# Cross-attention and stream-mixing kernel: small work moved between units of the order, and one step from VectorE to GpSimd

## The chip, the cores and the metric

The kernel runs on one core of one Trainium2 chip. The metric is the device time of one execution in microseconds (us); lower is better. Each figure given for a kernel is the median of several executions.

## What is computed

Shapes: x and the context are 8 batches x 512 rows (D) x 2048 columns (S), all float32. The reference, cut to what matters:

```python
x = x + tanh(g_xattn) * xattn(layernorm(x), ctx, mask)
x = x + tanh(g_ffn) * ffn(layernorm(x))

def xattn(qk, v, masks):            # per window of 128 columns, 8 heads of 32
    q, k, val = Wq @ qk + bq, Wk @ qk + bk, Wv @ v + bv
    attn = softmax(where(mask, q.T @ k / sqrt(32), -1e9))
    return (Wo @ gelu(attn @ val) + bo) * masks

def ffn(x):                         # per row: 4 streams of 512 columns
    x_norm = x * rsqrt(mean(x * x) + eps)
    res, pre, post = x_norm @ W_res.T + .., x_norm @ W_pre.T + .., x_norm @ W_post.T + ..
    H = sinkhorn_log(res, 50 iterations, tau=0.1)      # 4 x 4 per row
    H_pre, H_post = softmax(pre), softmax(post)
    H = (1 - g) * I + g * H
    y = (sum_n x_n * H_pre_n) @ W_branch
    return H @ x_streams + y * H_post
```

## The kernel before, in words

**Units.** The program is one loop over a counter g, written out for every engine by itself; the engines meet only at semaphores. A unit g is one window of 128 columns with one group of four heads. Eight units are a chunk (512 columns), and r = g % 8 is the place in it; four chunks are a batch of 32 units. Attention takes the units 0 to 255; 16 units ahead of them prepare the first chunks, and some 60 behind them finish the last batches. In each unit TensorE makes transposed scores, one or more bank products, the scores of the next unit and the values of the one before; VectorE takes the maximum over the scores (L1035) and divides values by denominators (L1043); ScalarE exponentiates (L838), copies banks and forms the inverse denominators (L845, L847).

**Bank products.** `banked_at(g)` says which products fall on a unit: q and k projections of the next chunk (r = 0 to 3), values v (r = 6 and 7), output projection o of the chunk before (r = 4 and 5), transpositions and logits of the finished chunk, `pre` (transposition of xpre). They take turns in four PSUM banks, and a product waits until the bank's earlier content was read.

**High and low parts.** bfloat16 products carry a high and a low part. ScalarE makes the high part (`hi_ctx` L793, `hi_x` L806 behind `norm_x` L799, `hi_gelu` L863), and GpSimd subtracts it from the float32 value (`split_ctx` L476, `split_x` L471, `low_gelu` L482). The tables HI_X_AT, LOW_X_AT, HI_CTX_AT and LOW_CTX_AT hold the unit r for each of the four row tiles.

**Iterations.** The Sinkhorn iterations of a batch run in the background of the batch behind it, 26 units long (SINK), two iterations or four halves a unit. A half is: GpSimd scales the exponentials by the last factor (`scale`, L536, writes kp), VectorE sums (L1166, writes ssum) and takes the reciprocal (L1167, writes sa or sv). `scale_at(..., 0..3)` on GpSimd and `half_at(..., 0..3)` on VectorE stand between the other work of the unit, and both queues are in order. For the last batch VectorE scales too (L1156). When the iterations end, VectorE's `coefficients` makes the mixing matrix cmat and the constant ccon from kp (L1181 to L1191). A pause in the middle (RETURN) brings the factors back into the logarithms.

**Output tiles.** Each of the four row tiles of a batch is finished beside the next batch's attention: load of x1t, `first_products` (ScalarE), `make_xpre` (VectorE, L1201), transposition, two halves of the branch product, then ScalarE's `first_out` (L926), VectorE's `add_stream` (L1213) and `add_y` (L1229), and the stores. BESIDE and BEHIND hold each part's distance in units from TILE_AT; BEHIND serves the last two batches.

**Queues.** SP issues nearly all loads and stores in the order of its own loop, among them the load of xc for the chunk after next, which waits for the last `split_x` of the chunk in front of it. GpSimd's own queue carries `add_x`, which adds x to the attention result while it is moved.

## Time and profile before

| what | us |
|---|---|
| median of three runs (1875.27 to 1878.99) | 1876.54 |
| profiled execution, its own time | 1877.37 |
| its span | 1875.6 |
| TensorE busy in the span | 1407.9 |
| VectorE busy | 1410.1 |
| ScalarE busy | 1056.0 |
| GpSimd busy | 757.3 |

The profile is one execution of the program as the hardware profiler recorded it. Busy is the time in which at least one instruction of an engine ran; PE is TensorE's matmuls, PEld its weight loads, DVE is VectorE, ACT ScalarE, POOL GpSimd, SP the DMA queue of SyncE. Times in rows count from the start of the span. Idle time in brackets is that of the engine just before the instruction, with what ended it. The first maximum of unit 0 starts at 72.0 us and that of unit 255 at 1583.0 us, so 293 us lie behind the attention.

### The profile page before, as it was taken

What the parts mean: (1) busy time and instruction counts of PE and PEld (TensorE: products, weight loads), DVE (VectorE), ACT (ScalarE), POOL (GpSimd) and SP (SyncE); (2) the same over time, 40 slices, a digit from 0 to 9 for tenths busy, and PEclk for the clock granted to TensorE, in tenths of its full rate; (3) what the DMA queues carried; (4) which work ended last, traced back from release to release, by engine and by line L of the source; (5) the groups of instructions that cost most, each with busy time, mean ns of one, the idle gap of its engine ahead of it and who ended that gap; (6) DMA issues with size and microseconds to landing.
All of it is one profiled execution on the core that took longest, in us unless ns stands there. A gap on an engine that the chain in (4) does not pass through costs nothing.

```text
span 1875.6 us, 35269 instructions
## 1 busy us (share of the span) xinstructions
PE 1407.9 (75%) x12323; PEld 859.3 (46%) x12448; DVE 1410.1 (75%) x3678; ACT 1056.0 (56%) x2017; POOL 757.3 (40%) x1237
## 2 busy tenths in 40 slices
PE   2779999888988888888888788888888886521223
PEld 0546656555645454455555454445555553320111
DVE  3334555666788897888888888888778887779997
ACT  3557776666766666665666666655666664311111
POOL 3224334555454544455454535454454524320000
PEclk9889999999989998999999898989989997656656
DMA  8457765566656666666656566665665443411123
GB/s 258 137 153 193 218 179 161 160 182 186 179 155 184 188 177 187 188 189 182 185 157 181 164 185 174 176 188 164 170 174 168 120 125 90 124 66 69 56 84 118
DMA packets 173920, 299.85 MB, mean 160 GB/s; under 512 B 23568, under 2 KB 74640, under 8 KB 169648
## 3 DMA queue, kind: packets, MB, share of 16 engines
q1 hardware_dynamic: 156336, 264.03, 45.3%
q0 software_dynamic: 17408, 33.56, 10.2%
q8 instruction: 100, 1.64, 0.4%
q14 instruction: 76, 0.62, 0.1%
HBM read 179.81 MB, written 67.11 MB: 132 GB/s over the span
## 4 chain that ended last, share of the span: by engine, by line
PE 43%; DVE 24%; ACT 10%; POOL 9%; issue 9%; DMA 2%; SPq 2%; DVEq 0%; ACTq 0%; POOLq 0%
PE pr L611 10%; PE pr L625 7%; PE pr L638 6%; PE f L740 4%; DVE ssum L1166 4%; PE av_ps L725 4%; POOL kp L536 4%; DVE otile_odd L1213 3%; POOL ctx_hl L476 3%; DVE negm L1035 2%; PE av_ps L729 2%; DVE sa L1167 2%; PE s_ps L698 2%; DVE otile_even L1213 2%; SPq L404 2%
## 5 line engine op out<-in xcount | busy, mean ns | idle before, releaser
L1166 DVE TENSOR_REDUCE ssum<-kp 128x16 f32<-128x64 f32 x768 | 181.9, 237 | 183.2 <-POOL kp L536 178.1
L476 POOL TENSOR_TENSOR ctx_hl<-ctx_raw,ctx_hl 128x512 bf16<-128x512 f32 x128 | 149.6, 1174 | 219.8 <-ACT ctx_hl L793 219.8
L611 PE MATMUL pr<-x_hl,wq 128*128 128x512 bf16 x708 | 193.0, 425 | 43.9 <-POOL x_hl L471 36.0
L536 POOL TENSOR_TENSOR kp<-ke,sa 128x64 f32<-128x64 f32 x343 | 136.6, 398 | 220.0 <-DVE sa L1167 220.0
L1035 DVE TENSOR_REDUCE negm<-s_ps 128x4 bf16<-128x512 f32 x256 | 166.9, 652 | 73.6 <-PE s_ps L698 72.1
L536 POOL TENSOR_TENSOR kp<-ke,sv 128x64 f32<-128x64 f32 x329 | 145.3, 442 | 187.7 <-DVE sv L1167 187.0
L698 PE MATMUL s_ps<-k_st,q_st 97*128 97x128 bf16 x1024 | 104.3, 226 | 152.8 <-DVE negm L1035 138.6
L611 PE MATMUL pr<-x_hl,wk 128*128 128x512 bf16 x736 | 186.0, 406 | 13.1 <-DVE logit L1101 8.0
L638 PE MATMUL pr<-o_sb,wo 128*128 128x512 bf16 x735 | 185.6, 389 | 11.5 <-POOL o_sb L482 6.9
L838 ACT ACTIVATE probs<-st_ps,key_bias 128x512 f32<-128x512 f32 x256 | 173.5, 678 | 30.5 <-PE st_ps L712 30.2
L471 POOL TENSOR_TENSOR x_hl<-xc,x_hl 128x512 bf16<-128x512 f32 x128 | 148.6, 1161 | 92.3 <-ACT x_hl L806 92.3
L625 PE MATMUL pr<-wv,ctx_hl 128*128 128x256 bf16 x1536 | 181.4, 276 | 3.2 <-DVE wv L1250 3.2
L845 ACT ACTIVATE lnden<-av_ps 128x128 f32<-128x128 f32 x256 | 71.1, 278 | 197.0 <-PE av_ps L729 191.9
L698 PEld LDWEIGHTS s_ps<-k_st,q_st 97*128 97x128 bf16 x1024 | 71.7, 100 | 223.1 <-DVE negm L1035 153.5
L625 PEld LDWEIGHTS pr<-wv,ctx_hl 128*128 128x128 bf16 x1536 | 148.0, 99 | 27.6 <-issue 10.0
L710 PE MATMUL st_ps<-q_st,k_st 96*128 96x128 bf16 x1024 | 148.3, 222 | 5.2 <-ACT probs L838 5.0
L685 PE MATMUL pr<-id_sb,xpre 128*128 128x128 f32 x128 | 24.5, 325 | 169.6 <-DVE xpre L1201 169.6
L1213 DVE SCALAR_TENSOR_TENSOR otile_even<-x1t_even,cmat,otile_even 128x512 f32<-128x512 f32 x192 | 147.7, 780 | 1.6 <-ACT otile_even L926 1.2
L1213 DVE SCALAR_TENSOR_TENSOR otile_odd<-x1t_odd,cmat,otile_odd 128x512 f32<-128x512 f32 x192 | 148.2, 794 | 0.7
L712 PE MATMUL st_ps<-id_bf,negm 128*128 128x128 bf16 x1024 | 147.4, 221 | 0.0
L725 PE MATMUL av_ps<-probs,v_t 128*32 128x128 f32 x2048 | 117.6, 303 | 36.2 <-DVE o_sb L1043 35.2
L611 PEld LDWEIGHTS pr<-x_hl,wq 128*128 128x128 bf16 x768 | 78.8, 108 | 141.7 <-issue 46.7
(142 smaller groups left out, 3047.1 us busy)
## 6 DMA issues: line engine op xcount, KB each, us to landing
xs<-in_dram SPq DMA_DIRECT2D x128, 256.0 KB, 4.6
xc<-in_dram SPq DMA_DIRECT2D x32, 1024.0 KB, 10.6
ctx_raw<-in_dram SPq DMA_DIRECT2D x32, 1024.0 KB, 6.8
x1c<-in_dram POOLq DMA_DIRECT2D x64, 512.0 KB, 9.3
x_dram<-x1c SPq DMA_DIRECT2D x32, 1024.0 KB, 4.9
q_st<-q_hl SPq DMA_DIRECT2D x384, 64.0 KB
k_st<-k_hl SPq DMA_DIRECT2D x384, 64.0 KB
x1t_even<-x_dram SPq DMA_DIRECT2D x16, 1024.0 KB, 5.8
```

What stands on the lines that cost most here:

```text
L471: nc.gpsimd.tensor_tensor(x_hl[:, G % 2, 1, t, :], xc[:, t, :], x_hl[:, G % 2, 0, t, :], ALU.subtract).then_inc(x_split, 1)
L476: ins = nc.gpsimd.tensor_tensor(ctx_hl[:, 1, t, :], ctx_raw[:, t, :], ctx_hl[:, 0, t, :], ALU.subtract)
L536: nc.gpsimd.tensor_tensor(kp[:], ke[:], v, ALU.mult).then_inc(kp_made, 1)
L611: ins = nc.tensor.matmul(bank(what)[:], w[:, a, t, i * P:(i + 1) * P], x_hl[:, G % 2, m, t, :], start=(t == 0 and a + m == 0), stop=(t == ...
L625: ins = nc.tensor.matmul(bank(what)[:, j * E:(j + 1) * E], ctx_hl[:, a, t, win], wv[:, m, t, :], start=(t == 0 and a + m == 0), stop=(t == ...
L638: ins = nc.tensor.matmul(bank(what)[:], wo[:, a, et, t * P:(t + 1) * P], o_part(G, et, m), start=(et == 0 and a + m == 0), stop=(et == ET ...
L698: ins = nc.tensor.matmul(s_ps[:, h * W:(h + 1) * W], q_st[0:ROWS + 1, G % 2, et, h, win], k_st[0:ROWS + 1, G % 2, et, h, win], start=True, ...
L725: nc.tensor.matmul(av_ps[rows, 0:W], v_t[:, G % 2, w, et * P + h * DH:et * P + (h + 1) * DH], probs[:, k % 2, h * W:(h + 1) * W], start=Tr ...
L838: nc.scalar.activation(probs[:, k % 2, :], st_ps[:], ACT.Exp, bias=key_bias[:, b, w:w + 1], scale=SCALE).then_inc(exp_done, 1)
L1035: nc.vector.tensor_reduce(negm[:, k % 2, :], s_ps[:].rearrange("p (h j) -> p h j", h=HPT), AX.X, ALU.max, negate=True).then_inc(max_done, 1)
L1166: cf.link(nc.vector.tensor_reduce(s_t, k, AX.X, ALU.add))
L1213: ins = nc.vector.scalar_tensor_tensor(out=otile[n % 2][:, i, :], in0=x1t[n % 2][:, j * C:(j + 1) * C], scalar=cmat[:, f % 2, t, i, j:j + ...
```

## The change

- ScalarE: high parts of ctx and x, `first_products` and `first_out` move from behind the unit's bank copies to a place ahead of them.
- GpSimd: low context parts come at r = 1, 2, 2, 3 instead of 0, 1, 1, 4, the first low part of x at r = 3 instead of 2, both low gelu parts at r = 4 instead of 3. Inside a unit the context split and the split of x change places, so that the split of x stands behind the third kp. The adds `add_x` move from r = 6 and 7 to r = 7 and the r = 0 that follows.
- `coefficients` runs on GpSimd in unit COEF_AT, the one behind the last iteration, with the row sum as two additions of halves and without the first scaling, which kp holds already. The semaphore for `pre` is now its own, and VectorE's next softmax, which reuses kp, waits for the coefficients.
- Bank products: v at r = 4 and 7, o at r = 5 and 6, logits at r = 5, `pre` two units behind xpre instead of one. Statistics at r = 2 and 5, the selection, the iterations and the output tiles one unit later, the pieces of the statistics of x at other units.

```diff
@@ -53,11 +53,11 @@
-HI_X_AT, LOW_X_AT = [1, 4, 5, 6], [2, 5, 6, 7]
-HI_CTX_AT, LOW_CTX_AT = [0, 0, 1, 1], [0, 1, 1, 4]
-
-T_AT, LOGITS_AT, SELECT_AT = [3, 3, 4, 4], 7, 8
-STAT_B_AT = [1, 3]
+HI_X_AT, LOW_X_AT = [1, 4, 5, 6], [3, 5, 6, 7]
+HI_CTX_AT, LOW_CTX_AT = [0, 0, 1, 1], [1, 2, 2, 3]
+
+T_AT, LOGITS_AT, SELECT_AT = [3, 3, 4, 4], 5, 9
+STAT_B_AT = [2, 5]
...
+COEF_AT = SINK_AT + len(SINK)
...
-BESIDE = dict(load=-8, first=-6, xpre=-5, pre=-4, branch_0=0, branch_1=1, out_0=-1, out_1=0,
+BESIDE = dict(load=-8, first=-6, xpre=-5, pre=-3, branch_0=0, branch_1=1, out_0=-1, out_1=0,
...
-TILE_AT = {(f, t): UNITS * (f + 1) + 53 + UPC * t for f in range(LAST_BESIDE + 1) for t in range(DT)}
+TILE_AT = {(f, t): UNITS * (f + 1) + 54 + UPC * t for f in range(LAST_BESIDE + 1) for t in range(DT)}
...
-    return [UNITS * (b - 1) + UPC * (p // 4 - 2) + 2 * (p % 4) for p in range(XS)]
+    return [UNITS * (b - 1) + UPC * (p // 4 - 2) + (1, 3, 4, 5)[p % 4] for p in range(XS)]
...
-                 6: [("v", G + 1, 0)], 7: [("v", G + 1, 1)]}.get(r, [])
-    if 0 <= G - 1 < NG and r in (4, 5):
-        made += [("o", G - 1, 2 * (r - 4)), ("o", G - 1, 2 * (r - 4) + 1)]
+                 4: [("v", G + 1, 0)], 7: [("v", G + 1, 1)]}.get(r, [])
+    if 0 <= G - 1 < NG and r in (5, 6):
+        made += [("o", G - 1, 2 * (r - 5)), ("o", G - 1, 2 * (r - 5) + 1)]
...
-                if r == 1 and 0 <= G - 2 < NG:
+                if r == 2 and 0 <= G - 2 < NG:
...
+            def coefficients(f):
+                pool.wait_ge(scale_made, HALVES * (f + 1))
+                flat = kp[:].rearrange("p t i j -> p t (i j)")
+                cp.link(nc.gpsimd.tensor_tensor(kp[:], kp[:], bcast(sv[:], 2, N), ALU.mult))
+                cp.link(nc.gpsimd.tensor_scalar(flat, flat, gt[:, 2:3], None, ALU.mult))
+                cp.link(nc.gpsimd.tensor_tensor(flat, flat, bcast(eye_g[:], 1, DT), ALU.add))
+                cp.link(nc.gpsimd.tensor_scalar(flat, flat, gt[:, 1:2], None, ALU.mult))
+                cp.link(nc.gpsimd.tensor_tensor(rows2[:], kp[:, :, :, 0:2], kp[:, :, :, 2:4], ALU.add))
+                cp.link(nc.gpsimd.tensor_tensor(rows1[:], rows2[:, :, :, 0], rows2[:, :, :, 1], ALU.add))
+                cp.link(nc.gpsimd.tensor_tensor(flat, flat, bcast(rb[:, f % 3, 3, :], 2, N * N), ALU.mult))
+                nc.gpsimd.tensor_tensor(ccon[:, f % 2], rows1[:], bcast(rb[:, f % 3, 6, :], 2, N), ALU.mult
+                                        ).then_inc(coef_ready, 1)
+                nc.gpsimd.tensor_tensor(cmat[:, f % 2].rearrange("p t i j -> p t (i j)"), flat,
+                                        bcast(eye_sb[:], 1, DT), ALU.add).then_inc(coef_ready, 1)
...
+                for ready in ffn_at(g, COEF_AT):
+                    coefficients(ready)
...
+                for H, t in at_step(g, -1, LOW_CTX_AT):
+                    split_ctx(H, t)
+                if 0 <= G - 1 < NG and r == 4:
+                    low_gelu(G - 1, 0)
+                scale_at(f, its, 2)
+                if 0 <= G - 1 < NG and r == 4:
+                    low_gelu(G - 1, 1)
                 for H, t in at_step(g, -2, LOW_X_AT):
                     split_x(H, t)
-                if 0 <= G - 1 < NG and r == 3:
-                    low_gelu(G - 1, 0)
-                scale_at(f, its, 2)
-                if 0 <= G - 1 < NG and r == 3:
-                    low_gelu(G - 1, 1)
-                for H, t in at_step(g, -1, LOW_CTX_AT):
-                    split_ctx(H, t)
                 scale_at(f, its, 3)
-                if 0 <= G - 1 < NG and r in (6, 7):
-                    add_x(G - 1, r - 6)
+                if 0 <= G - 1 < NG and r == 7:
+                    add_x(G - 1, 0)
+                if 0 <= G - 2 < NG and r == 0:
+                    add_x(G - 2, 1)
...
-                    act.wait_ge(coef_ready, 2 * f + 1)
+                    act.wait_ge(pre_ready, f + 1)
...
+                for H, t in at_step(g, -1, HI_CTX_AT):
+                    hi_ctx(H, t)
+                for H, t in at_step(g, -2, HI_X_AT):
+                    norm_x(H, t)
+                    hi_x(H, t)
+                for done, t in tiles_at(g, "first"):
+                    first_products(done, t)
+                for pair in range(2):
+                    for done, t in tiles_at(g, f"out_{pair}"):
+                        first_out(done, t, pair)
...
-                for H, t in at_step(g, -1, HI_CTX_AT):
-                    hi_ctx(H, t)
-                for H, t in at_step(g, -2, HI_X_AT):
-                    norm_x(H, t)
-                    hi_x(H, t)
...
-                for done, t in tiles_at(g, "first"):
-                    first_products(done, t)
-                for pair in range(2):
-                    for done, t in tiles_at(g, f"out_{pair}"):
-                        first_out(done, t, pair)
...
+                if f:
+                    dve.wait_ge(coef_ready, 2 * f)
...
-                if half and it == ITERS - 1:
-                    dve.wait_ge(scale_made, HALVES * (f + 1))
-                    coefficients(f)
```

ScalarE in unit 153 (r = 1 of a chunk with iterations). Before:

```order
L838 ACTIVATE probs<-st_ps,key_bias 128x512
L917 ACTIVATE xpt<-pr 128x512
L845 ACTIVATE lnden<-av_ps 128x128
L847 ACTIVATE rden<-lnden 128x128
L820 ACTIVATE q_hl<-pr,bq_sb 128x512
L793 ACTIVATE ctx_hl<-ctx_raw 128x512 x2
L799 ACTIVATE xc<-xc,ra 128x512
L806 ACTIVATE x_hl<-xc 128x512
```

With the change:

```order
L862 ACTIVATE probs<-st_ps,key_bias 128x512
L817 ACTIVATE ctx_hl<-ctx_raw 128x512 x2
L823 ACTIVATE xc<-xc,ra 128x512
L830 ACTIVATE x_hl<-xc 128x512
L844 ACTIVATE q_hl<-pr,bq_sb 128x512
L869 ACTIVATE lnden<-av_ps 128x128
L871 ACTIVATE rden<-lnden 128x128
```

The two high context parts (ctx_hl) and the normalization of x (xc, x_hl) stood behind the copy of the q bank and now stand ahead of it; xpt, the copy of `pre`, has left this unit.

GpSimd where two low context parts meet, units r = 1 and 2 before:

```order
L536 TENSOR_TENSOR kp<-ke,sv 128x64
L536 TENSOR_TENSOR kp<-ke,sa 128x64
L536 TENSOR_TENSOR kp<-ke,sv 128x64
L476 TENSOR_TENSOR ctx_hl<-ctx_raw,ctx_hl 128x512 x2
L536 TENSOR_TENSOR kp<-ke,sa 128x64
L536 TENSOR_TENSOR kp<-ke,sv 128x64
L536 TENSOR_TENSOR kp<-ke,sa 128x64
L471 TENSOR_TENSOR x_hl<-xc,x_hl 128x512
L536 TENSOR_TENSOR kp<-ke,sv 128x64
```

With the change (they are now in r = 2):

```order
L540 TENSOR_TENSOR kp<-ke,sa 128x64
L540 TENSOR_TENSOR kp<-ke,sv 128x64
L540 TENSOR_TENSOR kp<-ke,sa 128x64
L480 TENSOR_TENSOR ctx_hl<-ctx_raw,ctx_hl 128x512 x2
L540 TENSOR_TENSOR kp<-ke,sv 128x64
L540 TENSOR_TENSOR kp<-ke,sa 128x64
```

The pair ctx_hl stood between the third and the fourth kp of its unit and now stands between the second and the third.

GpSimd at the end of the last batch's work, with the change:

```order
L552 TENSOR_TENSOR kp<-kp,sv 128x64
L553 TENSOR_SCALAR kp<-kp,gt 128x64
L554 TENSOR_TENSOR kp<-kp,eye_g 128x64
L555 TENSOR_SCALAR kp<-kp,gt 128x64
L556 TENSOR_TENSOR rows<-kp 128x32
L557 TENSOR_TENSOR rows<-rows 128x16
L558 TENSOR_TENSOR kp<-kp,rb 128x64
L559 TENSOR_TENSOR ccon<-rows,rb 128x16
L561 TENSOR_TENSOR cmat<-kp,eye_sb 128x64
```

These nine (the coefficients) were VectorE's.

## Rows read from the trace of the kernel before

**Rows 1.** page, busy time of each engine (us, share of the span, count)
```profile
PE 1407.9 (75%) x12323; PEld 859.3 (46%) x12448; DVE 1410.1 (75%) x3678; ACT 1056.0 (56%) x2017; POOL 757.3 (40%) x1237
```

**Rows 2.** busy us of each engine by batch of 32 units; then granted clock, DMA share, GB/s
```profile
382.00:568.00 186.00, 160.28 (x1523) 99.94 (x1539) 136.53 (x399) 122.69 (x240) 94.11 (x167) 0.95 0.63 176
568.00:772.00 204.00, 171.71 (x1538) 105.05 (x1553) 172.77 (x447) 131.30 (x252) 100.11 (x167) 0.93 0.64 181
772.00:980.00 208.00, 175.17 (x1537) 105.96 (x1552) 172.61 (x447) 131.21 (x252) 100.31 (x167) 0.92 0.63 179
...
1391.00:1583.00 192.00, 156.93 (x1410) 96.35 (x1425) 154.15 (x408) 113.12 (x219) 81.74 (x142) 0.90 0.49 136
1583.00:1876.00 293.00, 91.37 (x287) 47.19 (x288) 248.17 (x689) 58.97 (x101) 36.03 (x82) 0.63 0.27 86
```

**Rows 3.** the same for the four chunks of the batch at 772 to 980 us
```profile
772.00:822.00 50.00, 42.65 (x378) 25.21 (x381) 42.47 (x108) 32.90 (x64) 24.22 (x38) 0.93 0.67 191
822.00:880.00 58.00, 46.48 (x391) 28.05 (x393) 47.30 (x136) 33.83 (x66) 31.45 (x64) 0.88 0.65 186
880.00:927.00 47.00, 41.81 (x391) 26.34 (x393) 39.59 (x89) 31.74 (x63) 17.10 (x22) 0.96 0.60 169
927.00:980.00 53.00, 44.23 (x385) 26.36 (x388) 43.26 (x117) 32.74 (x60) 27.54 (x45) 0.90 0.58 168
```

**Rows 4.** waits over the whole span: who for whom, us, times, longest
```profile
POOL ctx_hl L476 <- ACT ctx_hl L793: 219.8, 61, 19.2
...
DVE ssum L1166 <- POOL kp L536: 178.1, 304, 4.4
```

**Rows 5.** timeline, unit r = 1 of the chunk at 927 us
```profile
936.83 4.70 PE L611 MATMUL pr<-x_hl,wq 128*128 128x512 bf16 x11 [0.33 <-issue]
...
942.85 1.17 POOL L476 TENSOR_TENSOR ctx_hl<-ctx_raw,ctx_hl 128x512 bf16<-128x512 f32 x1 [4.62 <-ACT ctx_hl L793]
...
943.97 0.30 POOL L536 TENSOR_TENSOR kp<-ke,sa 128x64 f32<-128x64 f32 x1
...
944.30 0.27 DVE L1166 TENSOR_REDUCE ssum<-kp 128x16 f32<-128x64 f32 x1 [4.33 <-POOL kp L536]
...
945.45 0.40 PE L698 MATMUL s_ps<-k_st,q_st 97*128 97x128 bf16 x4 [0.87 <-DVE negm L1035]
```

**Rows 6.** timeline, VectorE in unit r = 3 of that chunk
```profile
954.40 0.22 DVE L1166 TENSOR_REDUCE ssum<-kp 128x16 f32<-128x64 f32 x1 [1.30 <-POOL kp L536]
```

**Rows 7.** timeline, collisions of GpSimd and VectorE in unit r = 4
```profile
959.94 0.66 DVE L1213 SCALAR_TENSOR_TENSOR otile_even<-x1t_even,cmat,otile_even 128x512 f32<-128x512 f32 x1
...
960.10 0.65 POOL L536 TENSOR_TENSOR kp<-ke,sv 128x64 f32<-128x64 f32 x1 [0.96 <-DVE sv L1167]
...
960.72 1.15 POOL L476 TENSOR_TENSOR ctx_hl<-ctx_raw,ctx_hl 128x512 bf16<-128x512 f32 x1
...
961.21 1.21 DVE L1213 SCALAR_TENSOR_TENSOR otile_even<-x1t_even,cmat,otile_even 128x512 f32<-128x512 f32 x1
```

**Rows 8.** timeline, end of the last batch's iterations
```profile
1810.38 0.23 DVE L1181 TENSOR_TENSOR kp<-ke,sa 128x64 f32<-128x64 f32 x1
...
1812.46 0.22 DVE L1191 TENSOR_TENSOR cmat<-kp,eye_sb 128x64 f32<-128x64 f32 x1
```

**Rows 9.** timeline, VectorE behind unit 256, two reciprocals 15 units apart
```profile
1584.19 0.25 DVE L1167 RECIPROCAL sa<-ssum 128x16 f32<-128x16 f32 x1
...
1667.25 0.25 DVE L1167 RECIPROCAL sa<-ssum 128x16 f32<-128x16 f32 x1
```

**Rows 10.** page, DMA issues: operation, count, KB each, us to landing
```profile
xc<-in_dram SPq DMA_DIRECT2D x32, 1024.0 KB, 10.6
```

**Rows 11.** timeline, load of xc, two context parts, first activation of the next unit r = 1
```profile
769.42 0.38 SPq L366 DMA_DIRECT2D xc<-in_dram  x1
...
776.00 1.13 ACT L793 ACTIVATE ctx_hl<-ctx_raw 128x512 bf16<-128x512 f32 x2
...
777.04 0.67 ACT L838 ACTIVATE probs<-st_ps,key_bias 128x512 f32<-128x512 f32 x1
```

More of the change, by code:

```diff
@@ L220, in program @@
         ones = sb("ones", [P, P])
[L221 removed]
+        spare = sb("spare", [P, 3])
         csum = sb("csum", [P, NL])
@@ L245, in program @@
         ccon = sb("ccon", [P, 2, DT, N])
+        rows2 = sb("rows2", [P, DT, N, 2])
+        rows1 = sb("rows1", [P, DT, N])
         pre = sb("pre", [P, 3, DT, N])
@@ L332, in program @@
         y_read = sem("y_read")
+        pre_ready = sem("pre_ready")
         coef_ready = sem("coef_ready")
```

22 lines of the change are left out of this document (4 added, 18 removed).

## The prediction, on record before the changed kernel ran

> **What bounds the kernel now.** I read the engine totals first, then the same totals batch by batch and chunk by chunk, then the waits, and last the timeline inside single units. The totals show two engines level: TensorE and VectorE are each busy for 75% of the span, ScalarE for 56%, GpSimd for 40% [rows 1]. By batch it is the same picture, sharper: in the batch at 772 to 980 us TensorE is busy for 175.2 and VectorE for 172.6 of 208 us [rows 2]. Neither is full, so some 33 us of this batch are lost in handshakes between them. The four chunks of that batch take 50, 58, 47 and 53 us for nearly equal TensorE work (42 to 46 us) [rows 3]; the loss sits in some units of a chunk and not in others.
>
> The list of waits names it. GpSimd waits 219.8 us for ScalarE's high part of the context, and VectorE waits 178.1 us for the scaled matrix kp that GpSimd makes [rows 4]. These are one chain, as unit r = 1 shows: TensorE's q projection starts at 936.83 and takes 4.70 us, ScalarE copies that bank at its end, and only behind this copy come the free activations that make the high context parts; GpSimd had waited 4.62 us for one of those, and since its queue is in order the kp behind the split starts at 943.97. VectorE stood still for 4.33 us, the maximum of the next unit was late, and TensorE idled another 0.87 us before its scores [rows 5]. So TensorE's own result, which nobody in the chain needed, holds TensorE. Unit r = 3 has a smaller copy of it (1.30 us) behind the low part of the gelu [rows 6]. In front of r = 1 TensorE works at the lower level: 11 matmuls took 4.70 us [rows 5], and the granted clock of the batch is 0.92 of the 2.4 GHz level [rows 2].
>
> **The change, part by part.**
> (1) ScalarE's free work ahead of bank copies, and low context parts a unit later (units 1, 2, 2, 3 instead of 0, 1, 1, 4), low gelu in unit 4. GpSimd then finds its operand ready each time. In the chunk at 927 to 980 us this removes 4.33 [rows 5] and 1.30 us [rows 6], and about 0.7 us of the same in r = 0, whose split moves away too (estimate: a sixth of the 4.33): 6.3 us. What is late next is kp itself. In r = 2 two splits of 1.17 us [rows 5] now stand between two kp; VectorE has a reduction (0.27) and one add (0.66) to cover them: 2 x 1.17 - 0.93 = 1.4 us of wait. Bounds: 0 if a bank read covers it, 2.3 if nothing does.
> (2) The splits of x move behind the third kp of their unit. What that costs is shown in r = 4: an add of VectorE with two SBUF inputs takes 0.66 us by itself and 1.21 us when it starts inside GpSimd's 1.15 us split; in the other direction kp takes 0.65 us beside the add and 0.30 us without it [rows 5, 7]. Before the change the split of x ran beside bank reads in units 5 to 7; now VectorE's add follows. Three units x 0.55 us = 1.7 us per chunk given back (bounds 0 and 7 x 0.55 = 3.9). The Trainium skill (SBUF — State Buffer, on the shared port pair) says that a VectorE instruction with two SBUF inputs and a GpSimd instruction that reads SBUF lock each other out until the first has ended. The trace agrees: the add ends 0.55 us behind the split's end. The rule speaks against this change, because GpSimd is freed to run just where VectorE runs.
> Net of (1) and (2) for this chunk: -6.3 + 1.4 + 1.7 = -3.2 us.
> (3) Coefficients on GpSimd. VectorE loses a chain of nine instructions, 1810.38 to 1812.68, 2.3 us [rows 8], seven times beside the last batch's. The same unit also held four adds of y and TensorE's two selections; the second selection and the statistics move on by one unit, which I put at 1.2 us (estimate, about half of the 2.3). So the chunk at 822 to 880 us wins 3.2 + 2.3 + 1.2 = 6.7 us. On GpSimd the nine take 0.30 us each [rows 5] and a handshake of about 0.1: some 3.6 us, in unit 17, where no kp is asked for: hidden. If GpSimd were late there, the softmax of unit 18 would wait, since it now asks for the coefficients.
> (4) Values at 4 and 7, output projection at 5 and 6, logits at 5, the transposition of xpre two units behind it instead of one: TensorE's heavy units are spread, and no wait for xpre is left at r = 0. TensorE's sum is unchanged. I count nothing beyond (1), as VectorE sets the pace then.
> The chunk at 772 to 822 us has a pause in its iterations, so I count -4.4 + 3.1 = -1.3 us; the chunk at 880 to 927 us has hardly any, and a third of its idle 47 - 39.6 us [rows 3] gives -2.5. The batch: -3.2 - 6.7 - 1.3 - 2.5 = -13.7 us. I take four fifths, -11 us, since new small waits appear when four engines move closer.
> Other batches, scaled by their load [rows 2]: the one at 568 us, whose row stands for the two behind 980 us as well, -10 each; 382 to 568 us, with few output tiles, -7; 218 to 382 us -2; the first 0; the last at 1391 us, -9. Sum: -11 - 30 - 7 - 2 - 9 = -59 us.
> (5) Behind unit 256, 293 us with VectorE busy for 248 [rows 2]. Iterations, tiles and statistics all start a unit later, so one iteration unit moves behind unit 256. Fifteen such units took 1667.25 - 1584.19 = 83.1 us, 5.5 us each [rows 9]. The coefficients of the batch before the last leave VectorE there (-2.3 us), and those of the last one, which ScalarE's first output waits for, take 3.6 us on GpSimd instead of 2.3 [rows 5, 8], +1.3. Sum +4.5 us.
> Total: -59 + 4.5 = -54.5 us against the profiled execution's 1877.4, so 1822.9; the median of the three runs lies 0.8 us lower: **1822 us**. The Trainium skill (GPSIMD Engine Reference, Engine selection) says to keep elementwise work on VectorE, as GpSimd is about twice as slow with two inputs. By it the last coefficients would cost 4.6 us instead of 3.6, 1 us more in the sum; for the small kp the row shows 0.30 us against VectorE's 0.23, so the trace does not agree at this size.
>
> **The rivals.**
> A, the forecast: the chain is broken, collisions and r = 2 give half of it back. For it: in units 5 to 7 of today's chunks, where no split waits for ScalarE, TensorE hardly idles. 1822 us.
> B, it all comes: no collision, no wait in r = 2. Then the chunk gains 6.3 instead of 3.2; with 3.1 us more in three chunks of four, over some five batches' worth, that is 37 us more at four fifths: 1785 us. Against it: the collisions in rows 7.
> C, the collisions cost their upper bound: 2.2 us more per chunk of this kind, and the wait in r = 2 grows to 2.3: 3.1 us more, so that a chunk hardly gains: 1822 + 37 = 1859 us. By the skill's lock (same page as above) this is the case that follows if every split meets an add; the sentences above say what rows show of it.
> D, slower: ScalarE now reaches the normalization of xc before its bank copies. Today it gets there late, because the copy of q waits for TensorE. The load of xc is issued at 769.42 and takes 10.6 us (median) to land, 780.0; the exponential of r = 1 starts at 777.04, and two context parts (1.13 us) now follow its 0.67 us: ScalarE is there at 778.8 [rows 10, 11]. The load is released by the last split of x, which now stands one kp later (about 1.5 us): 781.5, a wait of 2.7 us with the bank copy and the inverse denominators behind it, and VectorE's division and TensorE's values behind those. Over 27 chunks 73 us, if nothing covers it: 1895 us. It decides from 54.5 / 27 = 2.0 us exposed per chunk. Against it: GpSimd is no longer late, so the split comes earlier in time, and the division has most of a unit of slack.
> E, the pace is set by a loop that the chain only hides, and the time stays: 1877 us.
>
> **How the numbers follow.** A 0.60, own range 1803 to 1845; B 0.12; C 0.15; D 0.09; E 0.04. The range takes in A, C but for its worst part, and the near half of B: 1788 to 1860 us. A difference under about 0.2% (3.7 us) can't be told from none. Faster by more than that: A, B, C, 0.87; within it: E, 0.04; slower: D, 0.09.
>
> **What the changed profile would show.** (1) right: GpSimd's wait for ScalarE's ctx_hl near 0 in the main part and VectorE's wait of 4.3 us in r = 1 gone; wrong if it has moved to another split. (2) right: adds of about 1.2 us in units 5 to 7, and one wait of 1 to 2 us for kp in r = 2. (3) right: the unit with the coefficients no longer than its neighbours, nine small GpSimd instructions in unit 17 that nobody waits for. (5) right: the part behind unit 256 4 to 6 us longer. D would show as waits of ScalarE's xc for the DMA, with TensorE's values late behind them. The prediction is wrong if VectorE's busy time, not its idle time, takes what the waits gave back, beyond the 3.9 us per chunk of the bound.

## Result and profile after

| kernel | median, us | range | executions |
|---|---|---|---|
| before | 1876.24 | 1874.94 to 1878.99 | 6 |
| changed | 1868.22 | 1865.97 to 1870.83 | 6 |

The ratio is 0.9956, 95% interval 0.9943 to 0.9969: the change makes the kernel 8 us faster, where 54 were forecast. The sign was right, and 1868 lies outside the range of 1788 to 1860. The profiled execution's span is 1866.9 us.

Engine totals of the page, then the busy time by stretch (columns as in [rows 2]): first the same two stretches of time as there, then the four chunks of the batch that answers to [rows 3]. In the changed kernel the maximum of unit 255 starts at 1568.4 us and the span ends at 1866.9, so the stretch from 1583 us holds less of its work than it did before.

```profile
PE 1410.8 (76%) x12448; PEld 864.1 (46%) x12448; DVE 1410.7 (76%) x3606; ACT 1055.8 (57%) x2017; POOL 807.8 (43%) x1309
```

```profile
772.00:980.00 208.00, 177.01 (x1591) 108.18 (x1590) 176.49 (x447) 134.25 (x258) 109.05 (x179) 0.93 0.64 183
1583.00:1876.00 293.00, 88.13 (x224) 42.06 (x224) 236.54 (x649) 54.18 (x91) 38.34 (x91) 0.61 0.24 83
...
771.20:822.00 50.80, 42.27 (x382) 25.47 (x380) 42.59 (x108) 32.64 (x63) 25.69 (x38) 0.93 0.63 182
822.00:874.90 52.90, 42.87 (x383) 25.62 (x382) 45.76 (x126) 34.27 (x68) 30.64 (x56) 0.94 0.61 175
874.90:924.80 49.90, 43.84 (x398) 28.29 (x397) 40.78 (x92) 31.26 (x63) 23.53 (x40) 0.90 0.64 183
924.80:975.80 51.00, 44.64 (x396) 26.79 (x396) 44.43 (x116) 33.02 (x62) 28.42 (x45) 0.93 0.64 183
```

VectorE's total is that of [rows 1], and it holds 72 instructions less. The chunk with the coefficients went from 58 to 53 us and the one at 927 us from 53 to 51, but the light chunk, which had the least idle time [rows 3], went from 47 to 50. This batch takes 204.6 us where it took 208; three waits of the whole span show that the chain of [rows 4] was broken all the same:

```profile
PE s_ps L722 <- DVE negm L1060: 155.8, 74, 4.9
...
DVE ssum L1193 <- POOL kp L540: 123.8, 301, 2.5
...
POOL ctx_hl L480 <- ACT ctx_hl L817: 54.6, 14, 13.7
```

GpSimd's wait for the context parts fell from 219.8 to 54.6 us, VectorE's for kp from 178.1 to 123.8; TensorE's wait for the maxima rose from 138.6 (the line below, of the kernel before) to 155.8.

```profile
PE s_ps L698 <- DVE negm L1035: 138.6, 90, 4.0
```

The timeline of the units r = 1 to 3 of the same chunk (answers to [rows 5]):

```profile
936.58 0.63 DVE L1060 TENSOR_REDUCE negm<-s_ps 128x4 bf16<-128x512 f32 x1
...
937.95 2.72 POOL L480 TENSOR_TENSOR ctx_hl<-ctx_raw,ctx_hl 128x512 bf16<-128x512 f32 x2
...
938.96 0.60 PE L682 MATMUL pr<-id_sb,x1c 128*128 128x128 f32 x4
...
940.96 0.22 DVE L1193 TENSOR_REDUCE ssum<-kp 128x16 f32<-128x64 f32 x1 [1.30 <-POOL kp L540]
...
944.29 0.61 PE L722 MATMUL s_ps<-k_st,q_st 97*128 97x128 bf16 x4 [4.73 <-DVE negm L1060]
...
945.95 1.11 PE L682 MATMUL pr<-id_sb,x1c 128*128 128x128 f32 x4
```

In r = 1 VectorE no longer stands still before its maximum; the wait of 4.33 us is gone. In r = 2 the pair of context splits makes it wait 1.30 us, where 1.4 was forecast. TensorE then has too little of its own to do and idles 4.73 us, and its next four transpositions take 1.11 us instead of 0.60: the granted clock is 0.50 there, the lower of its two levels (1.2 GHz), and 1.00 at the earlier four.

For the comparisons below I measure a unit from one maximum of VectorE to the next, as the mean over the batches 3 to 6 (counted from 0) of the profiled execution, and sum eight units to a chunk:

| us per chunk, units | before | f1 | g2 | g3 | g4 | changed | e3 |
|---|---|---|---|---|---|---|---|
| 0 to 7 | 49.8 | 47.0 | 45.5 | 46.8 | 48.0 | 50.7 | 49.8 |
| 8 to 15 | 56.6 | 53.3 | 50.5 | 51.0 | 51.8 | 52.9 | 51.7 |
| 16 to 23 | 46.9 | 43.4 | 46.0 | 47.3 | 52.4 | 49.9 | 48.7 |
| 24 to 31 | 52.3 | 47.9 | 47.9 | 48.7 | 48.5 | 50.7 | 51.0 |
| batch | 205.6 | 191.5 | 190.0 | 193.8 | 200.8 | 204.2 | 201.1 |

### The profile page after: what moved, and what is told of

The parts are those of the page before. It is cut to its first block, busy times and chain, and to the rows that moved or that the text cites. A ratio compares the mean times of both kernels' runs of the same rounds, so it can differ in the third digit from the quotient of the medians.

```text
span 1866.9 us, 35401 instructions
## 1 busy us (share of the span) xinstructions
PE 1410.8 (76%) x12448; PEld 864.1 (46%) x12448; DVE 1410.7 (76%) x3606; ACT 1055.8 (57%) x2017; POOL 807.8 (43%) x1309
## 4 chain that ended last, share of the span: by engine, by line
DVE 34%; PE 26%; POOL 16%; issue 11%; ACT 5%; DMA 4%; SPq 3%; POOLq 0%; DVEq 0%; ACTq 0%
POOL kp L540 8%; PE pr L635 7%; DVE ssum L1193 6%; PE pr L649 4%; DVE sa L1194 3%; DVE negm L1060 3%; DMA xc<-in_dram 3%; DVE bn_b L1095 3%; DVE xpre L1210 3%; PE pr L682 3%; DVE otile_odd L1222 3%; POOL ctx_hl L480 3%; PE pr L662 2%; DVE otile_even L1222 2%; PE av_ps L749 2%
## 5 line engine op out<-in xcount | busy, mean ns | idle before, releaser
L1193 DVE TENSOR_REDUCE ssum<-kp 128x16 f32<-128x64 f32 x768 | 181.5, 236 | 128.9 <-POOL kp L540 123.8
L540 POOL TENSOR_TENSOR kp<-ke,sa 128x64 f32<-128x64 f32 x343 | 151.1, 441 | 273.3 <-DVE sa L1194 273.3
L540 POOL TENSOR_TENSOR kp<-ke,sv 128x64 f32<-128x64 f32 x329 | 151.2, 460 | 265.6 <-DVE sv L1194 258.7
L722 PE MATMUL s_ps<-k_st,q_st 97*128 97x128 bf16 x1024 | 106.6, 230 | 171.7 <-DVE negm L1060 155.8
L635 PE MATMUL pr<-x_hl,wk 128*128 128x512 bf16 x768 | 198.0, 413 | 0.0
L480 POOL TENSOR_TENSOR ctx_hl<-ctx_raw,ctx_hl 128x512 bf16<-128x512 f32 x128 | 153.5, 1223 | 54.6 <-ACT ctx_hl L817 54.6
L1222 DVE SCALAR_TENSOR_TENSOR otile_odd<-x1t_odd,cmat,otile_odd 128x512 f32<-128x512 f32 x192 | 163.9, 876 | 0.6
L1222 DVE SCALAR_TENSOR_TENSOR otile_even<-x1t_even,cmat,otile_even 128x512 f32<-128x512 f32 x192 | 158.2, 834 | 4.6 <-ACT otile_even L950 4.3
L709 PE MATMUL pr<-id_sb,xpre 128*128 128x128 f32 x128 | 34.0, 421 | 154.1 <-DVE xpre L1210 154.1
L764 PE MATMUL f<-wb,xpt 128*128 128x512 f32 x256 | 143.3, 696 | 5.5 <-ACT xpt L941 5.5
```

The costliest lines, as they stand in the source:

```text
L480: ins = nc.gpsimd.tensor_tensor(ctx_hl[:, 1, t, :], ctx_raw[:, t, :], ctx_hl[:, 0, t, :], ALU.subtract)
L540: nc.gpsimd.tensor_tensor(kp[:], ke[:], v, ALU.mult).then_inc(kp_made, 1)
L635: ins = nc.tensor.matmul(bank(what)[:], w[:, a, t, i * P:(i + 1) * P], x_hl[:, G % 2, m, t, :], start=(t == 0 and a + m == 0), stop=(t == ...
L722: ins = nc.tensor.matmul(s_ps[:, h * W:(h + 1) * W], q_st[0:ROWS + 1, G % 2, et, h, win], k_st[0:ROWS + 1, G % 2, et, h, win], start=True, ...
L1193: cf.link(nc.vector.tensor_reduce(s_t, k, AX.X, ALU.add))
L1222: ins = nc.vector.scalar_tensor_tensor(out=otile[n % 2][:, i, :], in0=x1t[n % 2][:, j * C:(j + 1) * C], scalar=cmat[:, f % 2, t, i, j:j + ...
```

## Experiments

Eighteen kernels. Those of one group (e, f, g, k1 to k4, k5 and k6) share a chip and its runs of the kernel before; differences in us between groups are of the medians, and the ratios with their 95% intervals say how far they hold. Many expectations missed; where a time lies outside what was expected, the text says so. Two theories stood at the start: the forecast gain never came, because the chain of waits was worth less than it looked; or it came, and other parts of the change took it back.

**e1 to e4: the changed kernel with one part altered.**

e1, low context parts one unit earlier:

```diff
-HI_CTX_AT, LOW_CTX_AT = [0, 0, 1, 1], [1, 2, 2, 3]
+HI_CTX_AT, LOW_CTX_AT = [0, 0, 1, 1], [1, 1, 2, 3]
```

> The changed kernel with the second low context part in unit r = 1 instead of r = 2 (LOW_CTX_AT 1, 1, 2, 3). Theory S (the split pair of r = 2 is what stands in the way: VectorE waits 1.3 us for kp there, TensorE has run ahead and starves 4.7 us before the scores of r = 3, its clock falls to 1.2 GHz): the wait of r = 2 goes, since r = 1 has 1.45 us of xpre work between the second and the third half, 1.0 us per chunk or more, over 28 chunks 25 to 50 us: 1820 to 1845 us. Theory P (TensorE's own load in r = 3 sets the time of r = 3 and 4): 1860 to 1870 us, the wait only moves.

Measured: 1867.11 us, ratio 0.9938 (0.9916 to 0.9960): no different from the changed kernel, inside the 1860 to 1870 of theory P. Unit 2 of a batch shrinks from 7.0 to 5.9 us and unit 1 grows from 6.0 to 7.0: the wait only moves. The pair in r = 2 is not the loss.

e2, `pre` moved from r = 3 to r = 4 (transposition three units behind xpre):

```diff
-BESIDE = dict(load=-8, first=-6, xpre=-5, pre=-3, ...
+BESIDE = dict(load=-8, first=-6, xpre=-5, pre=-2, ...
```

> The changed kernel with the transposition of xpre in unit r = 4 instead of r = 3 (pre=-2 in BESIDE), so that r = 3 holds two transpositions and k, and r = 4 two transpositions, pre and v. Theory P: the copy of the k bank comes 1.1 us earlier in r = 3, VectorE's wait of 1.65 us for it in r = 4 shrinks to under 0.6 us: 1.1 us in some 24 chunks, 1842 to 1850 us. Theory S: TensorE only starves a little longer before r = 4, 1863 to 1870 us.

Measured: 1861.73 us, 0.9912 (0.9891 to 0.9933). Some 6 us, the intervals of the ratios overlap, and the time lies between the two expectations; the place of `pre` is a small part at most.

e3, second half of the statistics at r = 4:

```diff
-STAT_B_AT = [2, 5]
+STAT_B_AT = [2, 4]
```

> The changed kernel with the second half of the statistics in r = 4 instead of r = 5 (STAT_B_AT 2, 4), so that GpSimd's last chain of small statistics work falls on unit 15 and no longer on unit 16, where the chain for the statistics of x stands too. Theory G (two chains of small GpSimd instructions between two kp cost 2.47 us once per batch): the wait in unit 16 halves, 1.2 us in 7 batches, 1858 to 1862 us. Theory that these chains are covered by TensorE's selections there: 1866 to 1870 us.

Measured: 1852.46 us, 0.9860 (0.9836 to 0.9885), 16 us less than the changed kernel and below both expectations. One small piece in the wrong unit costs twice what the whole change gained: unit 5 of a batch is 7.9 us long in the changed kernel and 5.5 here, while unit 4 grows from 6.3 to 7.7. STAT_AT follows this table, and so does where GpSimd computes the inverse roots. In the changed kernel those of x (ra) and of the streams (rb) both fall on unit 16:

```profile
875.37 0.63 POOL L500 TENSOR_TENSOR ra<-ra 128x4 f32<-128x4 f32 x1
...
878.52 0.20 POOL L534 TENSOR_TENSOR rb<-rb 128x4 f32<-128x4 f32 x1
878.67 0.30 POOL L540 TENSOR_TENSOR kp<-ke,sa 128x64 f32<-128x64 f32 x1
...
879.00 0.26 DVE L1193 TENSOR_REDUCE ssum<-kp 128x16 f32<-128x64 f32 x1 [2.47 <-POOL kp L540]
```

Eleven tiny instructions, 3.4 us in a row in front of a kp, and VectorE waits 2.47 us. In e3 unit 16 is 6.8 us long instead of 8.0, the 1.2 us that was expected. The batch as a whole shrinks by 3.1 us, so most of the gain lies in other units.

e4, coefficients on VectorE again, all else as changed:

```diff
-                for ready in ffn_at(g, COEF_AT):
-                    coefficients(ready)
...
+                if half and it == ITERS - 1:
+                    dve.wait_ge(scale_made, HALVES * (f + 1))
+                    coefficients(f)
```

> The changed kernel with the coefficients made by VectorE again, behind the last iteration of unit 16. By the term of the prediction (2.3 us seven times, on VectorE's path) it is 16 us slower, less 1.3 us that it gains at the very end: 1883 us. If the coefficients on GpSimd were nearly worthless (TensorE's selections set units 15 to 18): 1866 to 1870 us.

Measured: 1898.65 us, 1.0107 (1.0084 to 1.0129), slower than the kernel before and 15 us above the 1883 expected. Thirty us for a chain of nine instructions, seven times, is more than the chain lasts (2.3 us each). Unit 16 of a batch is 16.0 us long here and 8.0 in the changed kernel, while unit 18 falls from 10.7 to 8.2. The timeline of GpSimd and VectorE at the end of unit 16:

```profile
891.59 1.24 POOL L494 DMA_DIRECT2D x1c<-in_dram  x1 [0.19 <-issue]
892.43 4.90 POOL L480 TENSOR_TENSOR ctx_hl<-ctx_raw,ctx_hl 128x512 bf16<-128x512 f32 x4
...
896.88 1.56 POOL L475 TENSOR_TENSOR x_hl<-xc,x_hl 128x512 bf16<-128x512 f32 x1
```

```profile
892.88 5.65 DVE L1189 TENSOR_TENSOR kp<-ke,sa 128x64 f32<-128x64 f32 x1
898.57 0.23 DVE L1190 TENSOR_TENSOR kp<-kp,sv 128x64 f32<-128x64 f32 x1
```

The first product of the coefficients takes 5.65 us where it took 0.23 [rows 8]. It begins while GpSimd works through five splits in a row and ends with them. So about 5.4 us of the unit's 8 are this hold-up and 2.3 the chain itself. In front of the row stands the issue of `add_x` (x1c), 0.84 us ahead of the first split.

**f1 to f4: single parts on the kernel before, and one taken out of the changed kernel.**

f1, only ScalarE's order (`hi_ctx`, `norm_x`, `hi_x`, `first_products`, `first_out` ahead of the bank copies):

> The kernel before with ScalarE's part of the change alone: high parts of ctx and x, first_products and first_out ahead of the bank copies. The chain of the prediction (TensorE's q projection, bank copy, context part, split, kp) is cut by this alone: by its price (4.3 us in r = 1, 1.3 in r = 3 not, 28 chunks) 1876 - 3.5 x 28 x 0.8 = about 1800 us. Theory T (cutting the chain mostly moves the waiting: TensorE starves elsewhere, and an unblocked GpSimd holds VectorE up at the shared port): 1860 to 1880 us.

Measured: 1802.03 us, 0.9588 (0.9569 to 0.9607).

f2, only the low parts later:

```diff
-HI_X_AT, LOW_X_AT = [1, 4, 5, 6], [2, 5, 6, 7]
-HI_CTX_AT, LOW_CTX_AT = [0, 0, 1, 1], [0, 1, 1, 4]
+HI_X_AT, LOW_X_AT = [1, 4, 5, 6], [3, 5, 6, 7]
+HI_CTX_AT, LOW_CTX_AT = [0, 0, 1, 1], [1, 2, 2, 3]
```

> The kernel before with the low context parts at r = 1, 2, 2, 3 and the first low part of x at r = 3 alone. GpSimd then finds its operands ready without ScalarE's new order: the wait of 4.3 us in r = 1 goes too, about the same time as with ScalarE's part alone by both theories: near 1800 us by the price of the chain, 1860 to 1880 us by theory T.

Measured: 1813.64 us, 0.9661 (0.9638 to 0.9684): 63 us less than before, nearer to the price of the chain than to theory T.

f3, only `coefficients` on GpSimd, with the semaphores it needs:

> The kernel before with the coefficients on GpSimd alone, in the unit behind the last iteration. By the term of the prediction -2.3 x 7 + 1.3: 1861 us. By the run with the coefficients back on VectorE (30 us slower than the changed kernel, one of VectorE's nine instructions held for 5.65 us behind GpSimd's run of context splits) the move is worth much only where GpSimd's splits run free beside it; in the kernel before they wait for ScalarE there, so again about 1861 us, not 1846.

Measured: 1870.66 us, 0.9963 (0.9947 to 0.9978): 6 us less than before, where 15 were expected.

f4, the changed kernel with GpSimd's old order inside a unit:

```diff
                 scale_at(f, its, 1)
+                for H, t in at_step(g, -2, LOW_X_AT):
+                    split_x(H, t)
-                for H, t in at_step(g, -1, LOW_CTX_AT):
-                    split_ctx(H, t)
...
-                for H, t in at_step(g, -2, LOW_X_AT):
-                    split_x(H, t)
+                for H, t in at_step(g, -1, LOW_CTX_AT):
+                    split_ctx(H, t)
```

> The changed kernel with the old order inside a unit on GpSimd: the split of x behind the second kp, the context split behind the third. The collisions of the split of x with VectorE's adds (0.55 us in r = 3, 5, 6, 7) go, the pair of context splits in r = 2 stands behind an add and the statistics and costs less. If collisions and the pair are what the gain was given back to: -2.5 us per chunk, 1868 - 50 = 1815 us. If TensorE's pace is what is left: 1860 to 1868 us.

Measured: 1837.75 us, 0.9774 (0.9751 to 0.9798), 30 us less than the changed kernel and between the two expectations.

The first theory falls with f1: ScalarE's order alone brings 74 us, more than the whole forecast. Its four chunks, to be read beside [rows 3]:

```profile
755.70:802.00 46.30, 41.05 (x382) 24.90 (x380) 42.77 (x107) 32.42 (x63) 25.41 (x38) 0.96 0.74 205
802.00:855.60 53.60, 45.17 (x388) 27.21 (x386) 47.37 (x135) 33.02 (x65) 32.17 (x63) 0.90 0.69 197
855.60:899.40 43.80, 40.08 (x390) 25.10 (x390) 39.60 (x92) 32.23 (x64) 18.90 (x24) 1.00 0.63 181
899.40:947.40 48.00, 44.00 (x400) 26.89 (x399) 43.51 (x117) 32.64 (x61) 28.44 (x45) 0.93 0.67 192
```

VectorE's busy times are those of before, TensorE's are 0.2 to 1.7 us shorter at a higher granted clock; each chunk lost 3 to 5 us, the light one included. It is the chain: of the 14.1 us that a batch gains, 12.8 lie in the four units r = 1, where GpSimd had waited for the context parts (9.6, 9.6, 10.5 and 10.2 us before, 6.5, 6.5, 7.6 and 6.5 in f1). f1 moves four kinds of work at once, which were not tried apart, but f2 touches only the splits, brings 63 us and adds only 7 to g1: f1 and f2 break the same chain, each at one end.

**g1 to g4: the change put together step by step**, all four on one chip. g1 is f1 with the coefficients of f3; g2 adds the tables of f2; g3 adds GpSimd's new order (f4's edit the other way round); g4 adds values at 4 and 7, output projection at 5 and 6, logits at 5, the low gelu in unit 4, and the store and adds that go with them. What then still lacks is the shift by a unit of statistics, selection, iterations and tiles, with `pre` and the pieces of the statistics of x.

> ScalarE's new order (1802 us alone) and the coefficients on GpSimd, nothing else of the change; first of four kernels that build the change up step by step. Coefficients alone gave 6 us: 1796 us. If an unblocked GpSimd makes the coefficients' move worth more (VectorE held at the shared port), below 1790; if GpSimd's chain of nine stands in front of kp-free splits that TensorE waits for, 1802 to 1806.

> The same with the low context parts at r = 1, 2, 2, 3 and the first low part of x at r = 3. Both cures of the one chain together: if there was only one wait to remove, no further gain, within 5 us of the step before; if waits for ScalarE were still left in r = 0 and r = 1, 10 to 15 us less.

> The same with GpSimd's new order inside a unit (context split behind the second kp, split of x behind the third). By the run with the old order in the changed kernel (30 us faster) this step costs 25 to 35 us. If that order only hurts together with the new bank places, under 10 us.

> The same with v at r = 4 and 7, o at r = 5 and 6, logits at r = 5, low gelu at r = 4 and the adds of x at r = 7 and 0. What is left to the changed kernel behind this one is the shift of selection, statistics, iterations and tiles by a unit. The steps from 1802 to 1868 us must add up to 66: if TensorE's crowding in r = 3 and 4 is the cost, it comes with the shift (pre into r = 3) and not here, and this step is within 5 us; if the bank places themselves cost, 10 to 20 us here.

| step | us | ratio, interval | step's own |
|---|---|---|---|
| f1: ScalarE's order | 1802.0 | 0.9588 (0.9569 to 0.9607) | -74 |
| g1: + coefficients | 1804.5 | 0.9605 (0.9582 to 0.9629) | +2 |
| g2: + low parts later | 1797.1 | 0.9555 (0.9532 to 0.9578) | -7 |
| g3: + GpSimd's order | 1818.1 | 0.9675 (0.9652 to 0.9699) | +21 |
| g4: + banks, low gelu | 1847.7 | 0.9836 (0.9813 to 0.9859) | +30 |
| changed: + shift | 1868.2 | 0.9956 (0.9943 to 0.9969) | +21 |

The second theory stands: the gain came in the first three steps, and the last three give nearly all of it back. g2 beats both kernels. The first and the last row are from other chips than g1 to g4; by the ratios the steps are -77, +3, -9, +23, +30 and +22 us. g1 lies where the chain of nine on GpSimd was expected to stand in the way (1802 to 1806), g2's step of -7 lies between its two expectations, g3's is a little under the 25 to 35 expected, and g4's is above both of its expectations.

In g4 the loss sits in few units. Against g3, unit 17 grows from 11.4 to 14.4 us, unit 22 from 7.3 to 9.4, unit 4 from 7.0 to 8.2, and the last unit of each chunk (7, 15, 23, 31) from 5.4 or 5.6 to 6.3. GpSimd and VectorE in unit 17 of g4:

```profile
873.13 1.24 POOL L493 DMA_DIRECT2D x1c<-in_dram  x1 [0.25 <-issue]
873.97 4.92 POOL L479 TENSOR_TENSOR ctx_hl<-ctx_raw,ctx_hl 128x512 bf16<-128x512 f32 x4
878.44 1.56 POOL L474 TENSOR_TENSOR x_hl<-xc,x_hl 128x512 bf16<-128x512 f32 x1
```

```profile
873.32 0.75 DVE L1043 SCALAR_TENSOR_TENSOR q_hl<-pr,bq_sb,q_hl 128x512 bf16<-128x512 f32 x1 [1.99 <-ACT q_hl L843]
873.99 7.23 DVE L1219 SCALAR_TENSOR_TENSOR otile_odd<-x1t_odd,cmat,otile_odd 128x512 f32<-128x512 f32 x2
881.14 1.27 DVE L1093 BATCH_NORM_STATS2 bn_b<-x1c 128x6 f32<-128x512 f32 x2
```

It is e4's picture with another victim: two adds of 0.66 us take 7.23, and again `add_x` is issued 0.84 us ahead of the row. In unit 22 ScalarE is late: the copy of the values' bank and that of the logits now stand in front of the exponentials of the iterations:

```profile
906.21 0.57 ACT L900 ACTIVATE lgs<-pr 128x512 f32<-128x512 f32 x1
...
907.20 0.24 ACT L916 ACTIVATE ke<-zl 128x64 f32<-128x64 f32 x1
```

```profile
907.47 0.22 DVE L1191 TENSOR_REDUCE ssum<-ke 128x16 f32<-128x64 f32 x1 [2.83 <-ACT ke L916]
```

g3 waits 0.76 us at this place. In the changed kernel the picture differs, since its softmax and coefficients stand a unit later: no add of a batch 3 to 6 lasts over 1.72 us there. Its long units are 16 (8.0 us, 3.4 in g4) and 18 (10.7, 4.5 in g4), while 17 has 4.1 us and 22 has 4.8.

**k1 to k6: why the bank step costs 30 us.**

k1, g2 with g4's bank step and GpSimd's old order:

> ScalarE's order, coefficients on GpSimd, low parts later, and the moved banks and logits, but GpSimd's old order inside a unit (g2 plus the step of g4). In g4 unit 17 takes 14.4 us: VectorE's two adds last 7.23 us behind five GpSimd splits in a row. Pile-up theory (the bank step costs only because GpSimd's splits then run in a row beside VectorE's adds, which the new order in a unit brings): at most 10 us over g2, 1797 to 1807, and no add over 2.5 us. Bank theory (the places of values, output projection and logits cost by themselves, through TensorE's clock and waits): about 30 us over g2, 1822 to 1830.

Measured: 1841.16 us, 0.9786 (0.9772 to 0.9799), 44 us over g2. The bank step costs by itself, more than either theory gave it, so the pile-up theory falls as I had put it. Its second half, no add over 2.5 us, was wrong too: the two adds of unit 17 take 7.88 us here. The hold-up comes with the bank step, not with GpSimd's order. And from here to g4 that order costs only 7 us, where it cost 21 behind g2.

k2, g4 with values at 6 and 7 and output projection at 4 and 5, and with the store and the adds of x that go with them:

```diff
-                 4: [("v", G + 1, 0)], 7: [("v", G + 1, 1)]}.get(r, [])
-    if 0 <= G - 1 < NG and r in (5, 6):
-        made += [("o", G - 1, 2 * (r - 5)), ("o", G - 1, 2 * (r - 5) + 1)]
+                 6: [("v", G + 1, 0)], 7: [("v", G + 1, 1)]}.get(r, [])
+    if 0 <= G - 1 < NG and r in (4, 5):
+        made += [("o", G - 1, 2 * (r - 4)), ("o", G - 1, 2 * (r - 4) + 1)]
```

> g4 with the values at units 6, 7 and the output projection at 4, 5 again (with the store and the adds of x that go with them); logits at 5 and the low gelu in unit 4 stay. If the moved values and output projection carry the 30 us: about 1820. If the logits or the gelu do: about 1845.

Measured: 1831.13 us, 0.9727 (0.9709 to 0.9745). 17 us less than g4, between the two expectations. Unit 17 is 11.8 us and its adds 2.3 us for two: without the move no add is held up that long. But the move that k2 takes back includes that of `add_x` from r = 0 to r = 6, so k2 does not tell the banks' places from the place of this issue.

k3, g4 with `LOGITS_AT` 7:

> g4 with the logits at unit 7 again. The logits' bank lies in unit 21 of a batch, where g4's units 20 to 22 are 4 us longer than g3's (units 22: 9.4 against 7.3). If the logits' place does that: 15 to 20 us less than g4's 1848, some 1830. If not: 1845 to 1850.

Measured: 1847.01 us, 0.9814 (0.9794 to 0.9833). The logits cost nothing; unit 22 stays at 9.1, so its length is not theirs. In k2 it is 7.8, so it comes with values and output projection, which were not moved apart.

k5, g4 with both low parts of the gelu at r = 3:

> g4 with the low gelu in unit 3 of GpSimd again. Of g4's 30 us over g3 the places of values and output projection carry 16.5 (k2) and the logits none (k3). Unit 4 of a chunk is 8.2 us long in k2, k3 and g4 alike, against 7.0 in g3. If the gelu does that: about 12 us less than g4, some 1836. If the parts only cost together: 1845 or more.

Measured: 1857.02 us, 0.9893 (0.9871 to 0.9914): 9 us more than g4, not the 12 less that the gelu alone would give. The gelu's place depends on the banks': beside the moved banks unit 4 is the better, while beside the old ones gelu and logits together cost 13 us (k2 against g3; 10 by the ratios). So the parts cannot be priced one by one.

k6, g4 with a wait more, so that the splits of unit 17 start behind the adds:

```diff
+                if g >= 0 and u == 17 and b >= 3:
+                    pool.wait_ge(out_ready, 8 * (b - 3) + 7)
                 for H, t in at_step(g, -1, LOW_CTX_AT):
                     split_ctx(H, t)
```

> g4, and in unit 17 of the last five batches GpSimd waits for VectorE's first pair of output adds before it begins its splits. In g4 two adds take 7.23 us there beside five splits in a row, 1.3 to 1.5 us by themselves. Starvation theory (back-to-back GpSimd instructions keep the add from starting): an added wait makes the kernel faster, the adds at 0.7 us each, unit 17 some 4 to 5 us shorter, five times: 1822 to 1832 against g4's 1848. Rival (the unit waits for TensorE's q bank or for something else anyway, the long adds only fill the wait): 1845 or more.

Measured: 1840.90 us, 0.9807 (0.9788 to 0.9825). GpSimd and VectorE in unit 17:

```profile
878.77 4.49 POOL L479 TENSOR_TENSOR ctx_hl<-ctx_raw,ctx_hl 128x512 bf16<-128x512 f32 x4 [2.05 <-DVE otile_odd L1221]
```

```profile
877.27 1.41 DVE L1221 SCALAR_TENSOR_TENSOR otile_odd<-x1t_odd,cmat,otile_odd 128x512 f32<-128x512 f32 x2
...
879.79 0.71 DVE L1126 SCALAR_TENSOR_TENSOR logit<-csum,rb,pr 128x32 f32<-128x32 f32 x4
880.53 3.89 DVE L1136 SCALAR_TENSOR_TENSOR logit<-logit,rb,base_sb 128x32 f32<-128x32 f32 x4
```

The adds now run ahead of GpSimd's row and take 1.41 us for two again, so beside the row they lost the time. The wait also parts the row from the issue of `add_x`, which now lies 3.3 us ahead of it (875.48 us). But the row now meets the logits, which took 0.74 us and take 3.89. Unit 17 falls from 14.4 to 12.2 us, and the time lies between the two expectations. Its interval overlaps g4's, so that the wait makes the kernel faster is shown by the unit, not by the time.

k4, f1 with f2's tables, coefficients on VectorE:

> The kernel before with ScalarE's order and the later low parts only; coefficients stay on VectorE. Coefficients cost 2.5 us on top of ScalarE's order and 5.6 less than before alone, so their own effect here should be within 5 us of g2's 1797: 1792 to 1800. If GpSimd's pile-up of splits met the coefficient chain on VectorE as in the changed kernel (30 us), it would be 1810 or more.

Measured: 1806.95 us (1798.57 to 1812.33), 0.9611 (0.9593 to 0.9630), outside the 1792 to 1800 expected; g2 stays the best. By the medians the coefficients on GpSimd are thus worth 6 us on the kernel before, nothing on f1, some 10 on top of k4 (k4 to g2) and 30 in the changed kernel. The profiled executions of k4 and g2 differ by 1.5 us only, and show why the move brings so little: VectorE reaches unit 17 of this batch 3.6 us earlier in g2 (854.20 us) than in k4 (857.80), but TensorE, behind its selections, starts the q projection at 855.10 against 854.75. VectorE waits for its bank:

```profile
859.33 0.75 DVE L1041 SCALAR_TENSOR_TENSOR q_hl<-pr,bq_sb,q_hl 128x512 bf16<-128x512 f32 x1 [3.15 <-ACT q_hl L841]
```

Units 15 to 17 together take 20.1 us in k4 and 20.2 in g2.

## Why the prediction was wrong

**Term 1, the chain: right, and larger than forecast.** Taking the collisions out of the forecast (1.7 of the 3.1 us that made 37 in rival B, so 20 us), and the later statistics (1.2 us a batch, some 5 us in all), terms 1 and 3 say 59 + 20 - 5 = 74 us; g2, which has both, gained 79 against the 1876 of before. That this fits so well is partly luck. Without the coefficients (2.3 us a batch, some 13 in all) the chain was put at about 61 us, and k4, which has the chain without the coefficients, gained 69 (73 by its ratio) and f1 alone 74. The coefficients cost 2 us on top of f1 and brought 10 on top of k4, of which the two traces show 1.5. In single places the working holds: the wait in r = 2 is 1.30 us, 1.4 forecast, and the chunk with the pause, put at 4.4 without a working, gave 4.3 in g2. But the light chunk gave 3.5 us in f1 where I had put 2.5.

**Term 2, the collisions: the size right on g2, the mechanism in part.** 20 us forecast, 21 measured (g2 to g3). But the same edit costs 7 us behind k1 and 30 in the changed kernel (f4), so the match is of one neighbourhood. Adds of 1.21 us stand in units 5 and 6 as foreseen, none in unit 7, and those of unit 1 got shorter: all stretched adds of a batch together make 1.4 us of the 3.8 that g3's batch is longer. What the rest is was not tried.

**Term 3, the coefficients: wrong.** It was priced at 2.3 us each time, 16 in all; the runs gave 6, -2, 10 and 30. VectorE is free 2.4 us earlier in unit 15 (7.8 us in f1, 5.4 in g1), but unit 17 grows from 7.6 to 11.5, where TensorE, not VectorE, comes last. In the changed kernel most of the gain is that of avoiding the hold-up beside GpSimd's row (e4). Only the chain's own length came out: on GpSimd the last coefficients take 3.3 us, 3.6 forecast:

```profile
1800.36 0.30 POOL L552 TENSOR_TENSOR kp<-kp,sv 128x64 f32<-128x64 f32 x1 [135.97 <-DVE sv L1194]
...
1803.37 0.32 POOL L561 TENSOR_TENSOR cmat<-kp,eye_sb 128x64 f32<-128x64 f32 x1
```

**Term 4 is the step that failed: "I count nothing beyond (1), as VectorE sets the pace then."** It cost 30 us (g3 to g4), with the low gelu in unit 4 in it, and 44 on GpSimd's old order (g2 to k1). I looked at TensorE's sum alone. A moved bank product moves its reader too: the values' copy went to ScalarE's unit 4, where ScalarE already had a high part, two first outputs and two copies of xt, and the output projection's reads (1.40 us for two) went to VectorE's unit 7, beside four adds of y. VectorE is busy there for 6.16 of 6.33 us in g4 (the row below: the stretch, then PE, PEld, DVE, ACT, POOL), and the unit is 0.7 to 0.9 us longer than in g3 in every chunk, some 3.5 us of the 7.0 that a batch lost. TensorE is busy throughout too, but has the next scores done at 812.93 us, and VectorE comes to them at 815.47:

```profile
809.10:815.43 6.33, 6.33 (x70) 4.60 (x69) 6.16 (x17) 3.81 (x8) 3.46 (x6) 1.00 0.65 225
```

Unit 17 lost 3.0 us more, where VectorE's adds are held up beside five splits. That may not be the banks' doing: the change also moves the second `add_x` to r = 0, in front of these splits, which term 4 does not mention (the last section has what the traces say). k2 shows that values, output projection, store and `add_x` moved back together return 17 of the 30 us; how they divide, and how the rest divides between gelu and logits, stays open.

**The shift by a unit failed too.** I gave it 1.2 us a batch of gain and 5.5 us behind unit 256. The second was right (from the last maximum to the end it is 292.6 us before, 294.3 in g4, 298.5 changed: 5.9 more in all, 4.5 forecast). But ahead of it the shift costs some 17 us instead of saving: the second half of the statistics at r = 5, and with it two chains of inverse roots in one unit (e3 moves both and gains 16 us; which of the two weighs more was not tried apart, but the unit with the inverse roots gives 1.2 us of the 3.1 a batch). A cost counted nowhere: the first maximum comes at 75.8 us instead of 72.0; f1 has 75.1 and f2 72.1, so it is ScalarE's order that delays the start.

**The rivals.** C had the sign of what went wrong, with the wrong mechanism: the collisions cost 21 us on g2 and 30 in the changed kernel, not the 57 that its upper bound gives, and most of the loss came from elsewhere. D did not happen: ScalarE waits for the load of xc for 22.5 us in all (2.1 before), not 73. None of the cases held that the moves I counted as nothing or as a gain would cost 50 us. Nor did the sign of being wrong catch it: VectorE's busy time in a batch 3 to 6 rose from 171.7 to 172.8 us. As the coefficients' 2.3 us left it, what remains lasts about 3.4 us longer, under 1 us per chunk, far below the 3.9 of the bound; the rest of the loss is idle time.

## What to carry to other kernels

A move that leaves one engine's sum as it is has to be priced on every engine that reads what is moved, unit by unit: look for the unit where the reader is full. Where two engines are at 75% and all work in order, a small piece in a full unit costs more than it lasts (16 us for one half of the statistics). And a piece taken off an engine gains only where that engine comes last: ask who comes last once it is gone (the coefficients). Test the parts of such a change alone and then as a staircase: one part carried the whole gain, and three others took it back.
